# Attention with ALiBi beside a quantised linear layer: row blocks 22 ahead instead of 24, maxima turned by VectorE, another order at the beginning

## The reference

```python
xn  = (x - mean) / sqrt(var + 1e-5)
q   = (xn @ Wq.T)      # 16 heads of 16
k,v = (xn @ Wk.T), (xn @ Wv.T)   # 8 heads of 16, each used by two query heads
energy = q @ k.T - slope[head] * abs(i - j)
attn   = softmax(energy / 4) @ v                # per head, 1024 x 1024
att    = attn @ Wo.T + bo
x_scale = max(abs(xn)) / 127 per token          # xn rounded to int8, weights int8
lin    = (round(xn / x_scale) @ w8.T) * x_scale * w_scale + bias
out    = x + att + lin
```

## Time and profile before

| | |
|---|---|
| median of 3 runs | 1584.54 us (1584.26 to 1584.94) |
| the profiled execution | 1584.45 us |
| its span | 1582.7 us |
| TensorE matmul busy | 98% of the span |
| VectorE / ScalarE / GpSimd busy | 88% / 77% / 67% |
| granted TensorE clock, mean | 0.998 |

### The profile page before, as it was taken

How to read it: one execution, slowest core, us unless ns; L and a number is a source line. 1 busy time by engine, 2 the same in 40 slices (tenths; PEclk the granted TensorE clock), 3 DMA queues, 4 the chain that set the end, 5 groups by cost and what they waited for, 6 DMA issues and landing times.

```text
span 1582.7 us, 53404 instructions
## 1 busy us (share of the span) xinstructions
PE 1555.2 (98%) x22012; PEld 814.4 (51%) x22012; DVE 1398.9 (88%) x1665; ACT 1221.1 (77%) x2395; POOL 1063.1 (67%) x1596
## 2 busy tenths in 40 slices
PE   5899999999999999999999999999999999999999
PEld 5345554555555555545555545555545555444443
DVE  6999999889998989998989999989999888999981
ACT  4478788777788777788777787777787777888885
POOL 5567778777788776777777777777777766433332
PEclk9999999999999999999999999999999999999999
DMA  8322222333223332232332323332333321211111
GB/s 202 75 65 65 66 75 63 91 87 76 78 71 77 96 82 77 77 78 76 96 79 72 82 76 80 96 77 70 85 75 79 88 66 55 60 38 43 53 52 61
DMA packets 182183, 121.03 MB, mean 76 GB/s; under 512 B 99956, under 2 KB 154612, under 8 KB 181940
## 3 DMA queue, kind: packets, MB, share of 16 engines
q1 hardware_dynamic: 181940, 117.62, 28.2%
HBM read 81.40 MB, written 35.63 MB: 74 GB/s over the span
## 4 chain that ended last, share of the span: by engine, by line
PE 94%; DVE 3%; DMA 1%; issue 1%; POOL 1%; ACT 0%; SPq 0%; POOLq 0%; DVEq 0%; ACTq 0%
PE ps_ring L1218 28%; PE ps_pv L1283 28%; PE ps_row L1218 27%; PE ps_ring L1316 4%; PE ps_ring L1336 3%; DVE row_max L935 2%; PE ps_ring L1319 1%; PE ps_ring L1330 1%; PE ps_row L1308 1%; PE ps_ring L1233 1%; DMA parts_dram<-parts 0%; POOL token_first L632 0%; PE ps_row L1372 0%; DVE stats L852 0%; DMA att_t<-att_dram 0%
## 5 line engine op out<-in xcount | busy, mean ns | idle before, releaser
L935 DVE TENSOR_REDUCE row_max<-ps_row 128x1 f32<-128x1024 f32 x1024 | 1204.4, 1214 | 126.9 <-PE ps_row L1218 122.7
L1101 ACT ACTIVATE probs<-ps_ring 128x512 f32<-128x512 f32 x2048 | 1111.7, 599 | 213.8 <-PE ps_ring L1218 160.2
L1218 PE MATMUL ps_ring<-q,k 122*32 122x512 bf16 x8192 | 735.8, 379 | 1.2 <-ACT lin_first L1079 0.6
L1218 PE MATMUL ps_row<-k,q 120*32 120x512 bf16 x8192 | 640.6, 379 | 11.4 <-issue 5.7
L700 POOL TENSOR_TENSOR probs<-probs,near 128x256 f32<-128x256 f32 x512 | 377.3, 737 | 323.5 <-ACT probs L1101 275.7
L1283 PE MATMUL ps_pv<-probs,v_unit 128*32 128x512 f32 x4096 | 539.7, 593 | 0.0
L1218 PEld LDWEIGHTS ps_row<-k,q 120*32 120x32 bf16 x8192 | 249.2, 97 | 315.5 <-issue 160.0
L1218 PEld LDWEIGHTS ps_ring<-q,k 122*32 122x32 bf16 x8192 | 247.7, 95 | 303.7 <-issue 140.0
L1283 PEld LDWEIGHTS ps_pv<-probs,v_unit 128*32 128x32 f32 x4096 | 136.2, 110 | 72.0 <-POOL probs L700 0.4
L756 POOL CAST parts<-qk 128x384 bf16<-128x384 f32 x53 | 26.8, 505 | 95.7 <-ACT qk L1110 95.7
L1316 PE MATMUL ps_ring<-xn_t,wqk 128*128 128x128 f32 x636 | 79.6, 275 | 0.0
(11 more groups left out here) (82 smaller groups left out, 894.9 us busy)
## 6 DMA issues: line engine op xcount, KB each, us to landing
parts_dram<-parts SPq DMA_DIRECT2D x59, 288.0 KB, 3.2
token_b<-token_dram SPq DMA_DIRECT2D x53, 256.0 KB, 3.9
q<-parts_dram SPq DMA_DIRECT2D x128, 96.0 KB
q<-parts_dram SPq DMA_DIRECT2D x128, 64.0 KB
att_dram<-att_unit SPq DMA_DIRECT2D x126, 64.0 KB
att_t<-att_dram SPq DMA_DIRECT2D x56, 128.0 KB, 3.0
out<-out_tile SPq DMA_DIRECT2D x56, 128.0 KB, 1.7
xt<-x_t SPq DMA_DIRECT2D x53, 128.0 KB, 2.3
```

Of the source, the lines that this page charges most:

```text
L935: dve.tensor_reduce(row_max[:, par, e, qb:qb + 1], ps_row[qb % 2][:, :], AX_X, ALU.max, negate=True).then_inc(row_max_found, 1)
L1101: act.activation(probs[:, c % PBUFS, e, h * HALF:(h + 1) * HALF], ring_bank(u, c, e, h), ACT.Exp, scale=SCALE).then_inc(ring_freed, 1)
L1218: mm = pe.matmul(to[at, :], weights[:, at], moving, start=start, stop=stop)
```

## The change

**1. The maxima are turned by VectorE.** `turn_max` moves from TensorE to VectorE, as a transpose in blocks of 32 by 32 straight into SBUF. TensorE's 64 transposes, ScalarE's 64 copies and the ring's place for them go. The result has another layout, 128 partitions of 32, so `place_max` issues four DMAs of 32 by 32 instead of one of 32 by 128.

**2. Row blocks run 22 ahead.** `LEAD` = 22. The last row block of the next unit is now in slot 9 instead of 7, `split_max` moves from c = 3 to c = 4, and the turn stands between the reductions of slots 10 and 11. Unit 62 has row blocks in slots 0 to 9. `project_last` begins one chunk later.

**3. The beginning.** Reciprocal deviations are found four tiles ahead instead of three, and GpSimd no longer waits for VectorE's normalisation there. All `store_parts` come before any constant; `near_bias`, scales, biases and `wo` are loaded between and behind the sets. `first_others` stands behind row blocks 1, 2, 4, 6, 7, 9, 11, 12, 14, 16, 17, 19 and 21. TensorE waits for the last step of it only at the first `pv_block`. ScalarE's exponential of `near_bias` moves into the row blocks.

```diff
-WHOLE_SET = SET_LOADS + 1
+WHOLE_SET = SET_LOADS + P // TURN
+LEAD = SLOTS + 6
+OTHERS_BEHIND = [1 + (LEAD - 2) * k // 12 for k in range(PREP_AHEAD + 2)]
+        def row_at(n):
+            return n // SLOTS, n % SLOTS // BLOCKS, n % BLOCKS
+        def rows_of(u, i):
+            n = SLOTS * u + LEAD + i
+            return [row_at(n)] if n < SLOTS * UNITS else []
...
             def place_max(u, slot):
-                if u == 0:
-                    sp.wait_ge(max_t_ready, 1)
-                else:
-                    wait_freed(sp, u - 1, "maxima")
-                sp.dma_start(q_set[ROW_K:COL_K, slot, :, :].rearrange(
-                    "m e (a r) -> m (e a) r", r=P),
-                    neg_max_t[:, :]).then_inc(set_loaded[slot], 16)
+                sp.wait_ge(max_turned, u + 1)
+                for j in range(P // TURN):
+                    sp.dma_start(q_set[ROW_K:COL_K, slot, :, :].rearrange(
+                        "m e (a j r) -> m (e a) j r", j=P // TURN, r=TURN)[:, :, j, :],
+                        neg_max_t[j * TURN:(j + 1) * TURN, :]).then_inc(set_loaded[slot], 16)
...
             def find_rstd(t, par):
                 wait(pool, stats_ready, 2 * (t + 1))
-                wait(pool, xn_ready, t - 1)
+                if t >= PREP_AHEAD:
+                    pool.wait_ge(xn_ready, t - 1)
+                elif t >= 2:
+                    pool.wait_ge(rstd_ready, 2 * (t - 1))
...
-                    if c == 3 and not f["last"]:
+                    if c == 4 and not f["last"]:
                         split_max(u + 1)
...
+            def turn_max(u):
+                dve.wait_ge(max_split, 2 * (u + 1))
+                if u > 0:
+                    slot = (u - 1) % SETS
+                    dve.wait_ge(set_loaded[slot], set_count(u - 1, slot, WHOLE_SET))
+                dve.transpose(neg_max_t[:, :], neg_max[:, :, :].rearrange("p m a -> p (m a)")).then_inc(
+                    max_turned, 1)
...
                     for i in (2 * c, 2 * c + 1):
-                        if i < BLOCKS and f["row_heads"] >= 1:
-                            reduce_block(u + 1, (u + 1) % 2, 1, i)
-                        if i >= BLOCKS and f["row_heads"] >= 2:
-                            reduce_block(u + 2, u % 2, 0, i - BLOCKS)
+                        if i == 2 * SLOTS - LEAD + 1 and not f["last"]:
+                            turn_max(u + 1)
+                        for ru, e, qb in rows_of(u, i):
+                            reduce_block(ru, ru % 2, e, qb)
...
-            first_others(PREP_AHEAD + 1)
-            pe.wait_ge(max_t_ready, 1)
-            pe.wait_ge(first_lin_ready, PREP_AHEAD)
+            for n in range(SLOTS, LEAD):
+                first_row_block(*row_at(n))
+            pe.wait_ge(v_kept, PREP_AHEAD)
+            pe.wait_ge(xq_t_ready, PREP_AHEAD)
             pe.wait_ge(consts_loaded, CONSTS)
...
-                if i % 2 == 0 and 0 <= slots < BLOCKS:
-                    project_last(0, P, slots)
+                if i % 2 == 0 and 0 < slots <= BLOCKS:
+                    project_last(0, P, slots - 1)
```

More of the change, by code:

```diff
@@ L129, in ring_places @@
                 items += [(u, "qkv", t % PAIR) for t in f["made"]]
-            if c == 5 and not f["last"]:
-                items.insert(3, (u, "maxima"))
             for item in items:
@@ L538, in next_x @@
                 load_x(t)
-            for t in range(3):
-                store_parts(t, t % 2)
-            for dst, src in ((wscale, w_scale), (bias, bias_attn), (bias2, bias_lin)):
-                sp.dma_start(dst[:, :], src.unsqueeze(0).broadcast_to([P, EMBED])).then_inc(
-                    consts_loaded, 16)
-            store_parts(3, 1)
-            sp.dma_start(wo[:, :, :], wo_t.rearrange("(c p) n -> p c n", p=P)).then_inc(
-                consts_loaded, 16)
-            sp.dma_start(wo_last[:, :, :], wo_last_t).then_inc(wo_last_loaded, 16)
-            for t in range(4, BLOCKS):
+            for t in range(BLOCKS):
                 store_parts(t, t % 2)
@@ L554, in _ @@
                 store_parts(t, t % 2)
-            for u in range(1, SETS - 1):
-                load_set(u, u)
+            sp.dma_start(near_bias[:, :, :], diag.rearrange("g p n -> p g n")).then_inc(
+                near_loaded, 16)
+            load_set(1, 1)
+            for dst, src in ((wscale, w_scale), (bias, bias_attn), (bias2, bias_lin)):
+                sp.dma_start(dst[:, :], src.unsqueeze(0).broadcast_to([P, EMBED])).then_inc(
+                    consts_loaded, 16)
+            load_set(2, 2)
+            sp.dma_start(wo[:, :, :], wo_t.rearrange("(c p) n -> p c n", p=P)).then_inc(
+                consts_loaded, 16)
+            sp.dma_start(wo_last[:, :, :], wo_last_t).then_inc(wo_last_loaded, 16)
             for t in (PREP_AHEAD, PREP_AHEAD + 1):
@@ L674, in gather_v @@
                 pool.tensor_copy(v_unit[:, par, :, 0:HEAD_DIM], src).then_inc(v_unit_ready, 1)
-            for t in range(3):
+            for t in range(4):
                 find_rstd(t, t % 2)
             for t in range(PREP_AHEAD):
-                if t + 3 < PREP_AHEAD:
-                    find_rstd(t + 3, (t + 3) % 2)
+                if t + 4 < PREP_AHEAD:
+                    find_rstd(t + 4, t % 2)
                 find_low(t, t % 2)
@@ L705, in split_max @@
                 pool.wait_ge(row_max_found, BLOCKS * GROUP * (u + 1))
-                if u >= 2:
-                    wait_filled(pool, u - 2, "maxima")
+                pool.wait_ge(max_turned, u)
                 maxima = row_max[:, u % 2, :, :].rearrange("p e a -> p (e a)")
@@ L956, in _ @@
             split_first_max()
-            for qb in range(BLOCKS):
-                reduce_block(1, 1, 0, qb)
+            turn_max(0)
+            for n in range(SLOTS, LEAD):
+                ru, e, qb = row_at(n)
+                reduce_block(ru, ru % 2, e, qb)
             def turn_pv(u):
@@ L1139, in unit @@
                         for h in range(2):
-                            if (c, e, h) == (5, 1, 1) and not f["last"]:
-                                keep_maxima(u)
                             exps(u, c, e, h)
@@ L1245, in _, with first_row_block @@
             pe.wait_ge(w8_ready, 2)
+            def first_row_block(u, e, qb):
+                row_block(u, u, e, qb)
+                at = (GROUP * u + e) * BLOCKS + qb
+                if at in OTHERS_BEHIND:
+                    first_others(OTHERS_BEHIND.index(at))
             for e in range(GROUP):
@@ L1249, in _ @@
                 for qb in range(BLOCKS):
-                    row_block(0, 0, e, qb)
-                    if qb % 2 == 1:
-                        first_others((e * BLOCKS + qb) // 2)
+                    first_row_block(0, e, qb)
             wait_row_set(1, 1)
-            for qb in range(BLOCKS):
-                row_block(1, 1, 0, qb)
-                if qb == 1:
-                    turn_max(0, ps_ring[2][:, :]).then_inc(max_turned, 1)
-                if qb % 2 == 1:
-                    first_others((GROUP * BLOCKS + qb) // 2)
-            first_others(PREP_AHEAD + 1)
-            pe.wait_ge(max_t_ready, 1)
-            pe.wait_ge(first_lin_ready, PREP_AHEAD)
+            for n in range(SLOTS, LEAD):
+                first_row_block(*row_at(n))
+            pe.wait_ge(v_kept, PREP_AHEAD)
+            pe.wait_ge(xq_t_ready, PREP_AHEAD)
             pe.wait_ge(consts_loaded, CONSTS)
@@ L1288, in ahead_row_block @@
             def ahead_row_block(u, f, i):
[L1290 to L1295 removed]
+                for ru, e, qb in rows_of(u, i):
+                    if e == 0 and qb == 0:
+                        wait_row_set(ru, ru % SETS)
+                    row_block(ru, ru % SETS, e, qb)
                 slots = i // 2 + (u - UNITS + 2) * BLOCKS - BLOCKS // 2
[L1297 to L1298 removed]
+                if i % 2 == 0 and 0 < slots <= BLOCKS:
+                    project_last(0, P, slots - 1)
                 if i % 2 == 0 and slots >= BLOCKS + 2:
@@ L1347, in unit @@
                     col_half(u, c, 1, 0)
-                    if c == 5 and not f["last"]:
-                        turn_max(u + 1, take_bank(u, "maxima")).then_inc(ring_filled, 1)
                     if c >= 2:
```

46 lines of the change are left out of this document (12 added, 34 removed).

## The result

Four runs of the changed kernel took 1573.06 to 1574.65 us, median **1573.49**. Four runs of the kernel before beside them had a median of 1584.74. The ratio is 0.9928, with a 95% interval of 0.9911 to 0.9945, so the kernel became 11.3 us faster. Predicted were 1572.7.

A forecast was written before the change was run, and what follows sets the result against it. TensorE was taken to set the pace, except at the beginning, where VectorE's reductions did. Terms -7.1 + 0.3 - 1.9 - 2.4 + 0.8 + 0.2 - 1.6 = -11.7 gave 1572.7 us, range 1569 to 1579.

The forecast's parts named there:

- Part 1, -7.1: Turn leaves TensorE in units 0 to 61: 0.13 us back per even unit, 0.10 per odd, 7.1 us in all.
- VectorE, 0: VectorE's transpose behind slot 10's reduction takes 0.18 us, hidden before TensorE's next block; cost 0.
- SyncE, +0.3, with 0.65 us of room: Four DMAs per unit land 0.65 us before TensorE wants them; a few delayed four-packs cost 0.3 us.
- Rival B: Four DMAs come late, every unit waits at chunk 0; about 1620 or 1580.5 us; chance of costing whole gain 0.09.
- Enough: At the first columns, about 63 us, unit 0's turned maxima have already landed, at 61.5 to 62.
- Part 2, -1.9: Two row blocks leave the beginning, -2.3 us; unit 63 takes back 0.3 and unit 62 about 0.1; together -1.9.
- The -2.3: Two row blocks of 1.15 us each on VectorE leave the beginning, saving 2.3 us.
- Part 3, -2.4 for the first row block: Tile ring cut and loads moved, so unit 0's row loads start at about 30.7 us; -2.4, bounds -1.0 and -3.5.
- +0.8 for half clock and closer steps, +0.2 for split and turn: In early row blocks, steps at half clock starve VectorE, +0.8 us (0 to 1.5); its split followed by turn, +0.2.
- -1.6 at the end of the beginning: Between last row block and first columns VectorE's pause goes, saving 1.6 us; bounds 0 and -1.64.
- Rival C: Beginning gives little because loads or closer steps replace the waits cut; 1576.8 us, chance 0.12.

The follow-up runs named there:

- first profile: Profiled execution from the first measurement of the changed kernel, against the kernel before; span 1572.1 us, median of that measurement 1573.49 us.
- a1: The changed kernel measured and profiled once more, nothing altered; median 1572.95 us.
- e1: Changed kernel with the turn back on TensorE in chunk 6, ScalarE's copy and one DMA; 1578.34 us.
- e6: Changed kernel with VectorE turning the maxima twice, the first time into a tile nobody reads; 1572.86 us.
- e4: Changed kernel with each of the four DMAs for the turned maxima cut in two, so eight; 1662.56 us.
- e3: Changed kernel with row blocks 24 ahead again instead of 22; 1573.52 us.
- the pair on one chip: Changed kernel with unit 0's maxima placed ahead of the token load, row blocks 24 ahead against 22: 1574.17 against 1572.97 us.
- e7: Changed kernel with only the old ring of reciprocal deviations, three tiles ahead and GpSimd waiting for normalised values; 1576.25 us.
- e8: Changed kernel with only the old order of loads on SyncE, constants between the first tiles' stores; 1576.34 us.

## Why the prediction was right

The total was 1572.7 predicted and 1573.5 and 1572.95 measured. By the stages of the table the misses partly cancel:

| stage | predicted | first profile | a1 |
|---|---|---|---|
| up to the first row block | -2.4 | -3.7 | -4.3 |
| rows to columns (-2.3 + 0.8 + 0.2 - 1.6) | -2.9 | -2.6 | -2.4 |
| units and end (-7.1 + 0.3 + 0.4) | -6.4 | -6.2 | -6.3 |
| last stores | 0 | +1.9 | 0.0 |

The units, more than half of the gain, came out as worked out. That the whole is within 1 us is partly luck. Step by step:

- **Part 1, -7.1**: right in mechanism, a little large. The turn is gone from TensorE's line, chunk 5 went from 2.73 and 2.70 to 2.60, and undoing it (e1) costs 6.4 to 6.5 us in the units. Unit 42 became 0.10 shorter (20.92 to 20.82), not 0.13: over all even units chunk 5 lost 0.133 us, but the seven others grew from 2.597 to 2.602 each, and in e1 they are 2.597 again. Why, no run shows. The 390 ns that the Trainium skill ("VectorE: DVE Perf Modes", section "The three transpose paths") gives for a turn on TensorE would, by the estimate above, have made 24.6 us; 6.5 were measured.
- **VectorE, 0**: right; 0.20 us against my 0.18, and doubling it (e6) costs 0.3 us at most.
- **SyncE, +0.3, with 0.65 us of room**: the room was mis-sized. The issues take 0.70, 0.65, 0.61 and 0.61 us (medians of the first profile) rather than 0.72 each, and the last lands after 1.7 rather than 2.0. e4 measures it at 1.2 us. In the profiles of the changed kernel TensorE never waits for these DMAs in the units, so 0 in place of +0.3. Rival B is excluded at this place and its threshold shown. At the first columns the prediction says "Enough"; in a1 it was not, by 0.71 us.
- **Part 2, -1.9**: right in sign. The beginning gained about 2 us from it and the end lost up to 0.4 (e3; nothing in f2); the pair on one chip says 1.2. The -2.3 holds only together with the new steps: with the old ones 22 blocks save 0.3 to 0.5 us.
- **Part 3, -2.4 for the first row block**: too small, and the reason was incomplete. It came 3.7 to 4.3 us sooner, outside my own bound of -3.5. I made the ring the cause and the loads an addition to it; e7 and e8 show two limits of which each alone is enough to hold the whole gain back. Had only one been changed, I would have predicted a gain, and there would have been next to none. The loads of unit 0's rows started at 29.34 and 28.76 instead of 30.7.
- **+0.8 for half clock and closer steps, +0.2 for split and turn**: about right. 22 blocks took 27.0 and 26.4 us from first to last, against 25.36 in before up to its 22nd, +1.0 to +1.6. The granted clock was 0.50 from 34 to 38 us.
- **-1.6 at the end of the beginning**: about right. The gap from the last row block to the first columns went from 2.76 to 0.87 (first profile) and 1.65 (a1, 0.71 of it the wait for the four DMAs). VectorE's pause of 1.64 us went whole in the first profile, where it reduces ten blocks in a row from 56.81 on, and shrank to 0.55 in a1. VectorE's timelines of the first profile and, in the second fence, of a1:

```profile
56.81 11.36 DVE L937 TENSOR_REDUCE row_max<-ps_row 128x1 f32<-128x1024 f32 x10
```

```profile
62.97 4.62 DVE L937 TENSOR_REDUCE row_max<-ps_row 128x1 f32<-128x1024 f32 x4 [0.55 <-PE ps_row L1216]
```

  In unit 0 TensorE waits once for VectorE, which has tiles 11 and 12 in hand. This is no price of the change, since the kernel before has it too. TensorE's timelines, first profile of the changed kernel, then before:

```profile
71.56 0.61 PE L1216 MATMUL ps_row<-k,q 120*32 120x512 bf16 x8 [1.69 <-DVE row_max L937]
```

```profile
77.81 0.61 PE L1218 MATMUL ps_row<-k,q 120*32 120x512 bf16 x8 [1.78 <-DVE row_max L935]
```

First columns: predicted 63, measured 62.3 and 61.9. What the beginning gave more, the first profile's late stores took in its total, by chance. Rival C (beginning gives little, 1576.8) is what one gets with ring or loads left old: 1576.25 and 1576.34.

## What to carry to other kernels

Look for a second limit at the same place before pricing the removal of the first: a ring of waits and a slow landing can each hold a stage at the same time, and then neither edit shows much alone. It happened twice here, with ring and loads and with blocks and steps. When one DMA becomes several, price the last issue and its landing against the first instruction that wants them; this change was free with 1.2 us to spare and at twice the number cost 87 us. And a gain of 1 us in 1570 is seen in stages of the trace when single medians differ by as much from chip to chip.

## What the runs showed of the hardware

- A DMA of half as many elements (eight of 32 x 16 in place of four) takes SyncE's queue the same time to issue: 0.61 us from the third of a pack on in both, with medians of 0.69 to 0.70 and 0.65 for the first two. So for DMAs this small their number counts and not their size. Pieces of 64 bytes were issued no slower than those of 256 were (0.70 for the first of a pack against 0.72). By the Trainium skill ("DMA: Bandwidth & Descriptors", section "Specifications") both lie under the 512 bytes of a read-modify-write; whether one took place no run here shows.
- A fetch of instructions among the last stores goes with 2 us more for their landing (4.2 and 3.8 against 2.2), in 2 of 14 profiles. That the one causes the other is inferred. In the two profiles of one program the last fetch stands at 1568.01 and at 1563.47 us.
- TensorE's chunk in even units takes 2.597 us on average in before and e1, which have a turn on TensorE, and 2.602 in the changed kernel (chunks 0 to 6). The turn is not what decides it: in e4 it is 2.598 and in e6 2.598 (chunks 0 to 4) without one, and in odd units chunks 5 and 6 of the changed kernel take 2.597 and 2.598. It is open why.
